# Shared experts of a mixture-of-experts layer: gate and up products for 256 tokens at a time instead of 512

## The chip, the cores and the metric

The kernel runs on one core of a Trainium2 chip. The metric is the device time of one execution in microseconds (us); lower is better. The engines are TensorE (PE in the profile, with its weight loads as PEld), VectorE (DVE), ScalarE (ACT), GpSimd (POOL) and SyncE (SP, which only starts transfers here). One wide instruction stream per engine runs in order, and the engines meet through semaphores.

## The reference, cut to what matters

A decoder layer: a state-space block, a cross-attention block and a feed-forward block, with a layer norm after each, for 8 x 128 = 1,024 tokens of width 256. Only the feed-forward block is touched:

```python
# x: 1024 tokens x 256; 8 routed experts (2 per token) and 2 shared experts, inner width 640
gate = silu(x @ wg[e].T);  up = x @ wu[e].T;  out += comb[:, e] * ((gate * up) @ wd[e].T)   # routed
sgate = silu(x @ sg[j].T); sup = x @ su[j].T; out += (sgate * sup) @ sd[j].T                # shared, all tokens
```

## The kernel before, in words

`experts` works through `NG_` = 19 groups of tokens, numbered q. Groups 0 and 1 are the first shared expert on 512 tokens each; groups 2 to 16 are the 15 routed blocks of 256 tokens (`NBLK`, `BLK` = 256); groups 17 and 18 are the second shared expert on 512 tokens each (`HALF` = 512). Every group has `IT` = 5 slices of 128 of the inner width; slice i of group q is unit u = 5q + i.

Each float32 operand is split into a high and a low part, and `products` (lines 66 to 68) makes one product of three matmuls with stationary tiles of 128 x 128: high x high, high x low, low x high. The order of the stationary operands is high, high, low, so each matmul has its weight load.

For a unit, `gate_up(q, i)` makes the gate and the up product: 2 destinations x 2 slices of the contraction (`KT`) x 3 = 12 matmuls. In a shared group each of them has 512 moving columns and fills a PSUM bank of its own (`gate_of`, `up_of`), so a unit takes two banks and units alternate between two pairs of banks. In a routed block each has 256 columns, and gate and up share a bank. Then ACT applies silu (`gate`, L1946), DVE multiplies (`gated`, L2036), ACT rounds to the high part (`round_h`), DVE makes the low part (`rest_h`), and `down(q)` makes the output, 256 columns wide: 60 matmuls in a shared group, 30 in a routed block. A unit's matmuls wait (`f_h`) until the multiply of the last unit on the same banks is done.

PE's order for each q is written out by hand: `gate_up(q, 0)`, `gate_up(q, 1)`, `down(q - 1)`, turning of a block's tokens (`turn_block`), `gate_up(q, 2)` to `gate_up(q, 4)`. In group 0, `ranks` (2 small matmuls) stands in the place of `down`, and 28 spare matmuls of 256 columns stand before `gate_up(0, 4)`. The last `down(18)` comes at the end.

GpSimd does two things in this stage: 16 indirect transfers that scatter the tokens into the blocks (L1803), once `slot` is made from the output of `ranks`, and 16 indirect transfers that gather the routed results (L1811), once the last routed results are stored. The first run beside groups 0 and 1, the second beside groups 17 and 18.

Of the kernel before, what the change touches and what calls it, by code (L numbers as in the profile page):

```python
# [24 lines left out]
KT = DM // P  # L25
HALF = 512
# [26 lines left out]
BLK = 256  # L53
NBLK = (2 * TOK + E * (BLK - 1)) // BLK
# [7 lines left out]
def products(pe, out, lhs, rhs, first, last):  # L62


    (lh, ll), (rh, rl) = lhs, rhs
    pe.matmul(out, lh, rh, start=first, stop=False)  # L66
    pe.matmul(out, lh, rl, start=False, stop=False)  # L67
    return pe.matmul(out, ll, rh, start=False, stop=last)  # L68
# [1550 lines left out]
def before_on_bank(u):  # L1619

    def banks(v):
        return (2 * (v % 2), 2 * (v % 2) + 1) if shared(v // IT) else (v % 4,)

    for v in range(u - 1, -1, -1):
        if set(banks(v)) & set(banks(u)):
            return v
    return -1


def shared(q):  # L1630
    return q < 2 or q >= 2 + NBLK


def weights_of(q):
    return 0 if q < 2 else min(q - 1, NBLK + 1)
# [7 lines left out]
def experts(nc, a, scope, ident, x_tok, accm, wr, rank, s_router, xs, ys, s_zero, out):  # L1643
# [3 lines left out]
    with ExitStack() as layer:  # L1647
        sb, ps, sem = scope(layer)
        x_hi = sb("x_hi", [P, KT, TOK], F32R)
        x_lo = sb("x_lo", [P, KT, TOK], F32R)  # L1650
# [3 lines left out]
        gu_hi = [sb(f"gu_hi{i}", [P, 2, KT, FI], F32R) for i in range(2)]  # L1654
        gu_lo = [sb(f"gu_lo{i}", [P, 2, KT, FI], F32R) for i in range(2)]
# [7 lines left out]
        xT_hi = [sb(f"xb_hi{i}", [P, KT, BLK], F32R) for i in range(2)]  # L1663
        xT_lo = [sb(f"xb_lo{i}", [P, KT, BLK], F32R) for i in range(2)]
# [60 lines left out]
        def gate_of(u):  # L1725
            return bg[2 * (u % 2)][:, :] if shared(u // IT) else bg[u % 4][:, 0:BLK]

        def up_of(u):
            return bg[2 * (u % 2) + 1][:, :] if shared(u // IT) else bg[u % 4][:, BLK:2 * BLK]

        def width(u):
            return HALF if shared(u // IT) else BLK
# [6 lines left out]
        with nc.Block() as block:  # L1739
# [82 lines left out]
            def _(pe):  # L1822
                def gate_up(q, i):
                    u, w = IT * q + i, weights_of(q)
                    c, ws = w % 2, slice(i * P, (i + 1) * P)
                    if i == 0:
                        if q < 2:
                            pe.wait_ge(r_lo, 2 * q + 2)
                        elif not shared(q):
                            pe.wait_ge(f_xlo, q - 1)  # L1830
                    if before_on_bank(u) >= 0:
                        pe.wait_ge(f_h, before_on_bank(u) + 1)
                    for dst, s in ((gate_of(u), 0), (up_of(u), 1)):
                        if i == 0:
                            pe.wait_ge(w_gl[c], 2 * (w // 2) + s + 1)
                        for k in range(KT):
                            if shared(q):
                                tok = slice((q % 2) * HALF, (q % 2 + 1) * HALF) if q < 2 else \
                                    slice((q - NBLK - 2) * HALF, (q - NBLK - 1) * HALF)
                                x2 = (x_hi[:, k, tok], x_lo[:, k, tok])  # L1840
                            else:
                                x2 = (xT_hi[q % 2][:, k, :], xT_lo[q % 2][:, k, :])
                            mm = products(pe, dst, (gu_hi[c][:, s, k, ws], gu_lo[c][:, s, k, ws]), x2, k == 0, k == KT - 1)
                    mm.then_inc(f_g, 1)

                def down(q):
# [60 lines left out]
                for q in range(4):  # L1907
                    for k in range(KT):
                        for b in range(2):
                            mm = pe.transpose(turned[q][:, k * 256 + b * P:k * 256 + (b + 1) * P],  # L1910
                                              x_tok[:, 2 * q + b, k * P:(k + 1) * P], ident[:, :])
                    mm.then_inc(r_t, 1)
                pe.wait_ge(s_router, 32)
                for b in range(BATCH):
                    pe.wait_ge(r_f, b // 2 + 1)
                    for k in range(KT):
                        mm = pe.matmul(bd[0][:, b * E:(b + 1) * E], x_f[:, k, b * P:(b + 1) * P], wr[:, k, :],  # L1917
                                       start=(k == 0), stop=(k == KT - 1))
# [3 lines left out]
                for q in range(NG_):  # L1922
                    gate_up(q, 0)
                    gate_up(q, 1)
                    if q:
                        down(q - 1)
                    else:
                        ranks()
                    if 2 <= q <= NBLK:
                        turn_block(q - 1)  # L1930
                    gate_up(q, 2)
                    gate_up(q, 3)
                    if q == 0:
                        spare(pe, bd[1][:, 0:256], x_hi[:, 0, 0:P], x_hi[:, 0, 0:256], 28)
                    gate_up(q, 4)
                    if q == 1:
                        turn_block(0)
# [369 lines left out]
```

## Time and profile before

| | |
|---|---|
| runs | 784.43 us median of 3 (784.09 to 788.73) |
| profiled execution, its own time | 784.88 us, of which the span is 783.2 us |
| PE busy | 92% of the span, 5040 matmuls |
| shared gate and up products | 240 matmuls of 128x512 (20 units x 12) |
| feed-forward stage | about 487 to 783 us of the span |

Busy time is the time in which an engine had at least one instruction under way; neighbouring matmuls overlap, so the length of one says less than the distance between the starts of two. The granted clock (PEclk) is 1.00 where TensorE runs at 2.4 GHz and 0.50 where it runs at 1.2 GHz.

### The profile page before, as it was taken

The numbers are of one execution on the slowest core, as the hardware profiler recorded it, in microseconds if no ns is written. First come the engines' busy times: TensorE is split into PE (matmuls) and PEld (weight loads), VectorE is DVE, ScalarE is ACT, GpSimd is POOL, SyncE is SP. The second block draws the span as 40 slices with busy tenths as digits, with TensorE's granted clock in tenths as the row PEclk, the third lists the DMA queues.
The fourth block names the chain that finished last, engine by engine and source line by source line (L and its number), as shares of the span: only waits on it lengthen the run. The fifth ranks groups of instructions, "written<-read, shape, count | busy, mean of one in ns | idle before, by whom it ended". The sixth has DMA issues, their size and how long they took to land. (4 is left out here: it accounts for less than half of the span.)

```text
span 783.2 us, 15336 instructions
## 1 busy us (share of the span) xinstructions
PE 723.1 (92%) x5040; PEld 655.0 (84%) x5040; DVE 565.2 (72%) x1176; ACT 473.5 (60%) x1066; POOL 347.3 (44%) x512
## 2 busy tenths in 40 slices
PE   4998888878999999999999997998999999999975
PEld 3888666667889999999899986986999999999855
DVE  4864778877878888888878873665577777777346
ACT  4544766347777777777777772343477777776301
POOL 0002666588988787877787851053000000000341
PEclk9999999999999999999999999699999999999988
DMA  9002300100200000000600000266346766770121
GB/s 293 1 1 90 160 1 0 33 3 28 62 8 1 7 0 7 0 7 0 208 0 0 0 1 5 101 225 222 119 158 227 254 200 213 229 243 28 48 74 54
DMA packets 45940, 64.82 MB, mean 83 GB/s; under 512 B 4288, under 2 KB 34880, under 8 KB 45632
## 3 DMA queue, kind: packets, MB, share of 16 engines
q1 hardware_dynamic: 39936, 56.39, 21.6%
q0 software_dynamic: 1536, 4.20, 1.6%
q10 hardware_dynamic: 4416, 3.58, 1.6%
q8 instruction: 29, 0.48, 0.3%
q14 instruction: 23, 0.19, 0.1%
HBM read 53.14 MB, written 11.01 MB: 82 GB/s over the span
## 5 line engine op out<-in xcount | busy, mean ns | idle before, releaser
L1811 POOL DMA_INDIRECT gu_raw<-rows_out,slot x16 | 15.9, 995 | 203.1 <-DMA rows_out<-y_sb 198.5
L1946 ACT ACTIVATE sg<-bg 128x256 f32<-128x256 f32 (+1 forms) x95 | 40.8, 430 | 101.6 <-PE bg L68 87.5
L413 ACT ACTIVATE under_dt<-two,nb,under_raw 128x256 f32<-128x256 f32 x128 | 70.6, 561 | 45.5 <-DVE nb L496 45.5
L66 PE MATMUL bg<-xb_hi,gu_hi 128*128 128x256 f32 x300 | 86.9, 290 | 2.7 <-DVE xb_lo L2059 2.7
L2036 DVE TENSOR_TENSOR hf<-sg,bg 128x256 f32<-128x256 f32 (+1 forms) x95 | 45.0, 474 | 57.4 <-ACT sg L1946 53.8
L68 PE MATMUL bg<-xb_hi,gu_lo 128*128 128x256 f32 x300 | 85.6, 285 | 0.0
L67 PE MATMUL bg<-xb_lo,gu_hi 128*128 128x256 f32 x300 | 85.5, 285 | 0.0
L66 PE MATMUL two<-under_h 128*128 128x256 f32 (+1 forms) x208 | 66.9, 321 | 2.8 <-PEq L117 1.5
L594 POOL TENSOR_SCALAR under_dt<-under_dt,rec 128x256 f32<-128x256 f32 x128 | 62.7, 508 | 6.4 <-DVE rec L542 6.4
L66 PE MATMUL bd<-dn_hi,eh_hi 128*128 128x256 f32 x220 | 62.5, 284 | 1.9 <-issue 1.8
L67 PE MATMUL bd<-dn_lo,eh_hi 128*128 128x256 f32 x220 | 62.6, 285 | 1.6 <-issue 1.6
L68 PE MATMUL bd<-dn_hi,eh_lo 128*128 128x256 f32 x220 | 62.3, 283 | 1.5 <-issue 1.5
L66 PEld LDWEIGHTS bg<-xb_hi,gu_hi 128*128 128x128 f32 x300 | 58.2, 194 | 3.1 <-DVE xb_lo L2059 3.1
L2048 DVE TENSOR_TENSOR gu_lo<-gu_raw,gu_hi 128x1280 fp32r<-128x1280 f32 x34 | 50.5, 1488 | 12.6 <-ACT gu_hi L1961 12.6
L67 PE MATMUL two<-under_h 128*128 128x256 f32 (+1 forms) x208 | 58.7, 282 | 0.0
L68 PE MATMUL two<-under_h 128*128 128x256 f32 (+1 forms) x208 | 58.5, 281 | 0.0
L68 PEld LDWEIGHTS bg<-xb_hi,gu_lo 128*128 128x128 f32 x300 | 58.2, 194 | 0.0
L67 PEld LDWEIGHTS bg<-xb_lo,gu_hi 128*128 128x128 f32 x300 | 58.2, 194 | 0.0
L546 DVE TENSOR_TENSOR pT_lo<-two,pT_hi 128x1024 fp32r<-128x1024 f32 x32 | 39.2, 1225 | 21.2 <-ACT pT_hi L420 21.0
L1953 ACT ACTIVATE eh_hi<-hf 128x256 fp32r<-128x256 f32 (+1 forms) x95 | 43.2, 455 | 11.3 <-DVE hf L2036 9.7
L2042 DVE TENSOR_TENSOR eh_lo<-hf,eh_hi 128x256 fp32r<-128x256 f32 (+1 forms) x95 | 45.3, 477 | 2.9 <-ACT eh_hi L1953 0.3
L66 PEld LDWEIGHTS bd<-dn_hi,eh_hi 128*128 128x128 f32 x220 | 42.2, 192 | 2.9 <-issue 2.6
(294 smaller groups left out, 2556.5 us busy)
## 6 DMA issues: line engine op xcount, KB each, us to landing
gu_raw<-in_gu SPq DMA_DIRECT2D x17, 1280.0 KB
dn_raw<-in_dn SPq DMA_DIRECT2D x17, 640.0 KB
rows_in<-under_dt SPq DMA_DIRECT2D x1, 3840.0 KB, 13.1
rows_out<-y_sb SPq DMA_DIRECT2D x30, 128.0 KB, 2.1
x_blk<-rows_in ACTq DMA_DIRECT2D x13, 256.0 KB, 2.7
under_raw<-in_wq SPq DMA_DIRECT2D x1, 2048.0 KB, 7.7
under_raw<-in_wkv SPq DMA_DIRECT2D x1, 2048.0 KB, 12.3
under_raw<-in_wo SPq DMA_DIRECT2D x4, 512.0 KB, 4.0
```

The costliest lines, as they stand in the source:

```text
L66: pe.matmul(out, lh, rh, start=first, stop=False)
L67: pe.matmul(out, lh, rl, start=False, stop=False)
L68: return pe.matmul(out, ll, rh, start=False, stop=last)
L413: act.activation(self.prob[:, g % 2, h, :], self.b_s[:, h // 2, (h % 2) * MW:(h % 2 + 1) * MW], ACT.Exp, bias=self.nb[:, h:h + 1], scale=s ...
L546: dve.tensor_tensor(self.pT_lo[:, :, :], self.b_p[:, :, :], self.pT_hi[:, :, :].bitcast(F32), ALU.subtract).then_inc(self.a_plo, 1)
L594: pool.tensor_scalar(self.prob[:, g % 2, h, :], self.prob[:, g % 2, h, :], self.rec[:, h:h + 1], 1.0, ALU.mult, ALU.mult).then_inc(self.a_ ...
L1811: pool.indirect_dma_start(got[k][:, b, :], None, ys[:, :], bass.IndirectOffsetOnAxis(ap=slot[:, k, b:b + 1], axis=0)).then_inc(f_got[b], 16)
L1946: act.activation(sg[:, u % 3, 0:width(u)], gate_of(u), ACT.Silu).then_inc(f_sg, 1)
L1953: act.activation(h_hi[:, q % 2, i, 0:width(u)], hf[:, u % 3, 0:width(u)], ACT.Copy).then_inc(f_hhi, 1)
L2036: dve.tensor_tensor(hf[:, u % 3, 0:width(u)], sg[:, u % 3, 0:width(u)], up_of(u), ALU.mult).then_inc(f_h, 1)
L2042: dve.tensor_tensor(h_lo[:, q % 2, i, 0:n], hf[:, u % 3, 0:n], h_hi[:, q % 2, i, 0:n].bitcast(F32), ALU.subtract).then_inc(f_hlo, 1)
L2048: dve.tensor_tensor(gu_lo[c][:, s, :, :], gu_raw[c][:, s, :, :], gu_hi[c][:, s, :, :].bitcast(F32), ALU.subtract).then_inc(w_gl[c], 1)
```

## The change

In `gate_up`, the unit's tokens are cut into parts of `BLK` = 256 and the products are made part by part: for a shared unit first all of gate's contraction for the first 256 tokens (6 matmuls into the first half of gate's bank), then for the second 256, then the same for up. A shared unit then has 24 matmuls of 256 columns with 24 weight loads in place of 12 of 512 with 12. The banks, the semaphore increments, the waits, and all work of ACT, DVE, POOL and SP stay as they are. A routed unit has one part and is issued as before.

```diff
-                        for k in range(KT):
-                            if shared(q):
-                                tok = slice((q % 2) * HALF, (q % 2 + 1) * HALF) if q < 2 else \
-                                    slice((q - NBLK - 2) * HALF, (q - NBLK - 1) * HALF)
-                                x2 = (x_hi[:, k, tok], x_lo[:, k, tok])
-                            else:
-                                x2 = (xT_hi[q % 2][:, k, :], xT_lo[q % 2][:, k, :])
-                            mm = products(pe, dst, (gu_hi[c][:, s, k, ws], gu_lo[c][:, s, k, ws]), x2, k == 0, k == KT - 1)
+
+                        for part in range(width(u) // BLK):
+                            for k in range(KT):
+                                if shared(q):
+                                    at = (q if q < 2 else q - NBLK - 2) * HALF + part * BLK
+                                    x2 = (x_hi[:, k, at:at + BLK], x_lo[:, k, at:at + BLK])
+                                else:
+                                    x2 = (xT_hi[q % 2][:, k, :], xT_lo[q % 2][:, k, :])
+                                mm = products(pe, dst[:, part * BLK:(part + 1) * BLK],
+                                              (gu_hi[c][:, s, k, ws], gu_lo[c][:, s, k, ws]), x2, k == 0, k == KT - 1)
                     mm.then_inc(f_g, 1)
```

## Rows read from the trace of the kernel before

**Rows 1.** The page: PE's busy time, and the queue that carries instruction blocks.
```profile
PE 723.1 (92%) x5040; PEld 655.0 (84%) x5040; DVE 565.2 (72%) x1176; ACT 473.5 (60%) x1066; POOL 347.3 (44%) x512
...
q8 instruction: 29, 0.48, 0.3%
```
**Rows 2.** The tile bg: count, ns minimum/median/maximum, first and last start.
```profile
L66 PE MATMUL bg<-xb_hi,gu_hi x300: 278/283/415, 546.2 to 719.7; 128*128 128x256 f32 x150
...
L66 PE MATMUL bg<-x_hi,gu_hi x80: 387/389/790, 501.0 to 767.1; 128*128 128x512 f32 x80
```
**Rows 3.** Busy time by stretch: from:to, its length, engines, PEclk, DMA share, GB/s.
```profile
514.40:531.50 17.10, 16.47 (x105) 14.80 (x103) 11.33 (x17) 8.11 (x11) 13.74 (x12) 1.00 0.88 314
531.50:540.40 8.90, 8.10 (x35) 5.53 (x33) 3.53 (x6) 0.77 (x2) 4.79 (x5) 1.00 0.25 86
540.40:546.20 5.80, 3.48 (x16) 2.68 (x16) 3.26 (x7) 3.07 (x6) 0.00 (x0) 1.00 0.95 325
...
563.30:720.00 156.70, 156.70 (x1312) 156.70 (x1313) 120.14 (x197) 114.27 (x223) 0.00 (x0) 1.00 0.60 197
720.00:736.00 16.00, 16.00 (x88) 13.85 (x87) 5.22 (x10) 5.71 (x12) 0.00 (x0) 1.00 0.06 19
736.00:748.40 12.40, 12.40 (x78) 11.23 (x77) 8.50 (x16) 4.11 (x8) 9.63 (x10) 1.00 0.30 87
748.40:757.40 9.00, 3.77 (x15) 2.18 (x13) 2.55 (x6) 0.00 (x0) 6.30 (x7) 0.85 0.38 107
757.40:761.60 4.20, 4.17 (x10) 3.00 (x11) 1.51 (x4) 0.00 (x0) 0.00 (x0) 0.50 0.06 22
```
**Rows 4.** PE in order of time: wide products, then narrow ones, without a gap.
```profile
519.05 0.39 PE L68 MATMUL bg<-x_hi,gu_lo 128*128 128x512 f32 x1
...
525.17 0.39 PE L68 MATMUL bg<-x_hi,gu_lo 128*128 128x512 f32 x1
...
525.75 0.28 PE L66 MATMUL bd<-dn_hi,eh_hi 128*128 128x256 f32 x1
...
531.15 0.28 PE L66 MATMUL bd<-dn_hi,eh_hi 128*128 128x256 f32 x1
```
**Rows 5.** PE in order of time, groups 0 and 1, idle time in brackets.
```profile
517.11 0.50 PE L66 MATMUL bg<-x_hi,gu_hi 128*128 128x512 f32 x1 [0.63 <-DVE hf L2036]
...
533.06 0.48 PE L66 MATMUL bg<-x_hi,gu_hi 128*128 128x512 f32 x1
...
537.38 0.39 PE L68 MATMUL bg<-x_hi,gu_lo 128*128 128x512 f32 x1 [0.23 <-issue]
...
538.81 0.40 PE L67 MATMUL bg<-x_lo,gu_hi 128*128 128x512 f32 x1
...
540.50 0.50 PE L66 MATMUL bg<-x_hi,gu_hi 128*128 128x512 f32 x1 [0.36 <-DVE hf L2036]
```
**Rows 6.** POOL in order of time: first and last indirect transfer, scatter and gather.
```profile
514.38 2.53 POOL L1803 DMA_INDIRECT rows_in<-x_tok,slot  x1 [26.26 <-DVE slot L2147]
...
536.54 0.96 POOL L1803 DMA_INDIRECT rows_in<-x_tok,slot  x1 [0.30 <-issue]
...
736.03 0.99 POOL L1811 DMA_INDIRECT gu_raw<-rows_out,slot  x1 [198.53 <-DMA rows_out<-y_sb]
...
755.58 0.95 POOL L1811 DMA_INDIRECT gu_raw<-rows_out,slot  x1 [0.30 <-issue]
```
**Rows 7.** PE in order of time, beginning and end of the stretch at 1.2 GHz.
```profile
757.43 0.79 PE L66 MATMUL bg<-x_hi,gu_hi 128*128 128x512 f32 x1 [0.33 <-issue]
...
761.59 0.40 PE L66 MATMUL bg<-x_hi,gu_hi 128*128 128x512 f32 x1
```
**Rows 8.** The chain that ended last, where group 1 ends and group 2 begins.
```profile
543.31 0.25 PE bg L68
...
546.21 0.39 PE bg L66
```
**Rows 9.** DMA queues in the stretch 563.3 to 720: packets, MB, share.
```profile
q8 instruction: 11, 0.18, 0.5%
```

## The prediction

> **What bounds the kernel now.** I read the page first: PE is busy for 92% of the span [rows 1], so the question is what PE's own stream costs. The tile view then says which instructions the change touches: the wide products, 80 for each of three lines, 240 in all [rows 2]. Third came a table by stretch [rows 3]. In the routed stretch PE and its weight loads are busy for all of the 156.70 us. The same holds for 720 to 748.4. PE is the bound there, and a longer PE stream moves the end one for one. Three stretches look different. In 531.5 to 540.4 PE handles 35 matmuls in 8.90 us; in 748.4 to 757.4 it handles 15 in 9.00 us; in 757.4 to 761.6 the granted clock is 0.50. The reader should see that the first two lie under the last part of POOL's two runs of indirect transfers, 514.38 to 537.50 and 736.03 to 756.53 [rows 6], and that PE's gaps there are put down to "issue": it waited for no semaphore. Where group 1 hands over to group 2, the chain runs from PE's last product through ACT and DVE and back to PE in 2.9 us [rows 8], so a later end of group 1 is passed on in full.
>
> **The plain price.** The length of one matmul (389 ns wide, 283 ns narrow [rows 2]) is no price, because neighbours overlap. The distance of starts is. Wide: from 519.05 to 525.17 there are 27 steps, 6.12 / 27 = 0.2267 us. Narrow: from 525.75 to 531.15 there are 45 steps, 5.40 / 45 = 0.1200 us [rows 4]. Two narrow ones cost 0.2400, so each wide product that is cut costs 0.0133 us more, and 240 cost 3.2 us. The weight loads double from 240 to 480 and add nothing to this: the narrow rows already have one load each.
> The Trainium skill, TensorE: Matmul & The Clock Gate, section Back-to-back issue gap, gives columns / 2.4 + 2.5 ns for a single stream of matmuls; an estimate by that page is 2.5 ns for each cut and 0.6 us for all 240. The trace differs: its fixed part is five times as large, with a weight load for each matmul. I go by the trace.
>
> Two corrections. First, at 517.11 PE waits 0.63 us for DVE's multiply [rows 5], whose engine is behind because it makes the tokens' places from the output of `ranks`. The 24 wide products ahead of `ranks` move that chain by 0.32 us; the 48 ahead of 517.11 move PE by 0.64. So about 0.3 of 0.64 us arrives. Second, the products at clock 0.50 (10 in 4.20 us [rows 3], 757.43 to 761.59 [rows 7]) take 0.42 us each; at half the clock two narrow ones should cost the same, so 0.1 us falls away. The plain price is 3.2 - 0.3 - 0.1 = 2.8 us. DVE and ACT have the same work and gain slack. The 0.36 us wait at 540.50 [rows 5] could hide a little more; I leave that in the range.
>
> **What the plain price leaves out: instructions.** PE's instruction count in the shared gate and up products doubles, from 480 to 960 with the weight loads, and the question is whether they arrive as fast as PE could use them. The routed stretch says yes when POOL is quiet: 1312 matmuls in 156.70 us, 8.4 per us [rows 3]. While POOL issues indirect transfers, the rows say no. Between 533.06 and 540.50 PE does the 24 wide products of two units [rows 5]; less the closing wait and the tail before it, that is about 6.9 us against 24 x 0.2267 = 5.4. PE pauses in a rhythm of 1.43 us (537.38, 538.81 [rows 5]), with about 5 products in each: 24 / 6.9 = 3.5 products per us. The narrow rate wanted by the change is 8.3. In the gather it is worse: 13 or so in 9.00 us, 1.4 per us [rows 3].
> Why did neither pause begin with the indirect transfers? A store that is emptied explains it. Before 531.5 PE had done about 101 products since 514.4 (14 spare, 36 wide, 51 narrow); before 748.4 it had done 77 since 736.0 (30 wide, 47 narrow: 30 x 0.2267 + 47 x 0.12 = 12.4). With 3.5 per us arriving, 101 - 60 = 41 and 77 - 43 = 34 came out of the store. The two agree roughly, which is why I take this seriously; it is an inference, since no row shows the store.
>
> *Scatter.* From 517.1 to 540.4 PE did 36 wide, 60 narrow and 24 wide: 120 products. The same place now needs 72 + 60 + 48 = 180. Upper bound: the store is emptied in both kernels, the same 120 arrive, and 60 narrow ones are left when the supply recovers: 60 x 0.12 = 7.2 us. Lower bound: the shortage begins at 531.5 whatever PE has used. Then PE reaches 117 of 132 by 531.5, 33 more arrive by 540.4, and 30 are left: 3.6 us. The last unit of the group adds 0.2.
> *Gather.* Before, 90 products by 757.4. Now 120 are needed. Upper bound: the same 90 arrive, 30 x 0.12 = 3.6 us. Lower: the shortage begins at 748.4 again, by then 103 of 120 are done, 13 arrive, 4 are left: 0.5 us.
> *Elsewhere.* 0.3 us before the scatter; 720 to 736 holds (16.00 - 30 x 0.12) / 0.2267 = 55 wide products, 0.7 us; the end, 27 warm ones, 0.4 us.
> *Clock.* A narrow product occupies PE half as long as a wide one, so at 3.5 per us PE is idle for more than half of the time, as it was before the clock fell to 0.50 at 757.4. A second such stretch after the scatter would cost up to 16 narrow products at about 0.21 instead of 0.12 us, 1.5 us; at least nothing, because the kernel before already has a slow start after 546.2.
>
> Sum: low 0.3 + 3.8 + 0.7 + 0.5 + 0.4 = 5.7 us; high 0.3 + 7.4 + 0.7 + 3.6 + 0.4 + 1.5 = 13.9 us. Between them I take 10: the agreement of the two stores speaks for the upper half, and an argument from two stretches for some caution. 784.9 + 10 = 794.9 for the profiled execution; it lies 0.45 us above the median, so 794.5 us. This case's own range is 790 to 799.
> The Trainium skill, Runtime: NRT & Kernel Launch, section Instruction fetch mechanics, says that instructions are streamed in blocks ahead of use and that this is mostly hidden. By that page the forecast would be the plain price. The routed stretch agrees with it; the two stretches under POOL's transfers don't, unless the pauses have another cause.
>
> **Rivals.**
> *A. Only the plain price.* The pauses are tied to POOL's transfers in time and not to how many instructions PE uses; then 784.4 + 2.8 = 787.2 us, 786 to 789.5. For it: under the 30 wide products after 736.0 nothing pauses, though the transfers run. Against it: five products for each 1.43 us looks like a count. Chance 0.28.
> *B. The forecast*, 790 to 799. Chance 0.50.
> *C. The scatter starves as hard as the gather did.* At 1.4 per us from the start of a shortage at about 525, 15 us bring 21 products where the upper bound has 53, 32 x 0.12 = 3.8 us on top of 13.9: about 801 to 804. For it: the gather's rate is a row. Against it: the scatter's own rate is 3.5. Chance 0.08.
> *D. Faster: the gather's shortage moves away.* Instructions come in blocks on queue 8, 11 for the 1312 + 1313 of the routed stretch [rows 3, 9], about 240 in each. The change puts 240 more instructions ahead of the gather's groups and 240 into them. If the shortage arises where PE comes to the end of a block while POOL is busy, then what decides is whether such an end lies between 736 and 757; groups 17 and 18 shift by about one block, which nearly restores the old place, so only a difference of some tens of instructions could move it out. If it does, the 13 products of 9.00 us take 1.6, and the 10 at half clock take 2.3 instead of 4.20: 9.3 us less, 784.4 + 2.8 - 9.3 = 778 us. With only a part of it gone the time is 778 to 784. Chance 0.10.
> *E. The change does nothing to PE*, because the second load of the same weights or the split of the bank hides something: no row points to it, and the time would be 784. Chance 0.04.
>
> **How the numbers follow.** A measurement of this kernel tells a change of about 1% from none, 776.6 to 792.3 us. Below it lies a part of D, 0.03. Within: A, E, most of D, and about 0.13 of B, 0.51. Above: 0.37 of B, and C, 0.46. The likeliest single case is still B, with 794.5. The range has to take in A and B, and runs from 785.5 to 800; it leaves out C, D, E and edges, 0.2.
>
> **What would show it.** In the profile after: 480 narrow matmuls from x_hi and x_lo on bg, 0.120 us apart where nothing else happens (if not, the plain price is wrong); 31 packets on queue 8 instead of 29; PE's first pause after 514 well before 531, in the middle of `down(0)` or earlier, with "issue" as its releaser (if it comes at 531 to 532, the store is wrong and the low sum stands; if there is none, A); the end of group 1 4 to 9 us later than 543.6 on PE; the routed stretch of 156.70 us unchanged; from the gather's first transfer to the end of `down(17)` 1 to 4 us longer. The prediction is wrong if PE issues 8 products per us beside POOL's transfers, or if the pauses move with block ends rather than with what has been used.

## The result and the profile after

The changed kernel takes 800.11 us (median of 4 runs, 795.65 to 805.16), the kernel before 784.26 us on the same chip. The ratio is 1.0177 with a 95% interval of 1.0125 to 1.0229, that is 13.9 us slower (784.3 x 0.0177). The four runs fall into two pairs, 795.65 and 796.31, 803.9 and 805.16, and the median lies between them. The profiled execution is one of the longer pair, 805.16 us with a span of 802.4 us; its 19.2 us over the span before are more than the typical difference. Three kernels of the experiments had one execution each at a much lower granted clock (976.93, 822.39 and 825.17 us), which is left out of their times and ratios here.

The page, PE and the queue of instruction blocks [rows 1]:

```profile
PE 732.1 (91%) x5280; PEld 674.9 (84%) x5280; DVE 564.1 (70%) x1176; ACT 473.5 (59%) x1066; POOL 344.3 (43%) x512
...
q8 instruction: 30, 0.49, 0.3%
```

The tile bg, the products on x_hi [rows 2]; there were 80 of 512 columns for each line:

```profile
L66 PE MATMUL bg<-x_hi,gu_hi x160: 277/283/415, 502.8 to 786.6; 128*128 128x256 f32 x160
```

Busy time by stretch, as in [rows 3]. The columns are from:to, length, PE, PEld, DVE, ACT, POOL (busy us and instructions), granted clock, DMA share, GB/s.

```profile
516.90:529.20 12.30, 11.94 (x99) 11.74 (x98) 6.00 (x12) 2.98 (x5) 9.86 (x9) 1.00 0.84 292
529.20:541.10 11.90, 4.84 (x17) 3.58 (x16) 0.52 (x1) 0.00 (x0) 7.10 (x8) 0.63 0.57 211
541.10:559.30 18.20, 15.92 (x114) 15.67 (x113) 11.44 (x17) 8.96 (x13) 0.00 (x0) 0.86 0.46 150
...
576.70:733.20 156.50, 156.50 (x1312) 156.50 (x1311) 119.83 (x196) 114.19 (x222) 0.00 (x0) 1.00 0.60 197
...
751.00:762.00 11.00, 10.09 (x81) 9.64 (x80) 4.53 (x8) 2.35 (x4) 8.56 (x9) 1.00 0.32 96
762.00:771.50 9.50, 2.39 (x8) 1.46 (x7) 5.51 (x11) 1.75 (x3) 6.98 (x7) 0.63 0.34 97
771.50:780.00 8.50, 6.65 (x38) 6.83 (x39) 1.51 (x4) 0.00 (x0) 0.00 (x0) 0.61 0.06 18
```

Its second row is to be read first: in 529.2 to 541.1 PE handled 17 matmuls in 11.9 us. Before, it handled 35 in 8.9. POOL's indirect transfers, first and last of the scatter and of the gather [rows 6]:

```profile
516.89 2.53 POOL L1803 DMA_INDIRECT rows_in<-x_tok,slot  x1 [26.46 <-DVE slot L2149]
...
537.48 0.96 POOL L1803 DMA_INDIRECT rows_in<-x_tok,slot  x1 [0.31 <-issue]
...
750.97 0.99 POOL L1811 DMA_INDIRECT gu_raw<-rows_out,slot  x1 [212.53 <-DMA rows_out<-y_sb]
...
770.16 0.95 POOL L1811 DMA_INDIRECT gu_raw<-rows_out,slot  x1 [0.30 <-issue]
```

PE in order of time. The two pauses that answer to [rows 5] and [rows 7], with the idle time in brackets:

```profile
529.07 0.28 PE L66 MATMUL bd<-dn_hi,eh_hi 128*128 128x256 f32 x1
529.74 0.28 PE L67 MATMUL bd<-dn_lo,eh_hi 128*128 128x256 f32 x1 [0.38 <-issue]
...
534.02 0.37 PE L67 MATMUL bd<-dn_lo,eh_hi 128*128 128x256 f32 x1 [1.04 <-issue]
...
541.14 0.37 PE L67 MATMUL bd<-dn_lo,eh_hi 128*128 128x256 f32 x1 [0.43 <-issue]
...
545.59 0.41 PE L67 MATMUL bd<-dn_lo,eh_hi 128*128 128x256 f32 x1
...
760.97 0.38 PE L68 MATMUL bd<-dn_hi,eh_lo 128*128 128x256 f32 x1 [0.43 <-issue]
...
773.73 0.37 PE L68 MATMUL bd<-dn_hi,eh_lo 128*128 128x256 f32 x1 [1.03 <-issue]
```

The first pause beside the scatter now comes after the 7th product of `down(0)`, 12.8 us after POOL's first transfer. Before, the hesitation began near the 51st, 17 us after. From 541.3 to 546.0 products are about 0.213 us apart, with no idle time between them: the instructions come again, but the granted clock is still 0.50.

Where the 19.2 us are. Each row below is the distance between four starts read from the tile view and PE's order of time: first shared product, first routed product, first product of group 17, last matmul, and from that to the end of the span.

| us | first product at | groups 0, 1 | routed | groups 17, 18 | tail |
|---|---|---|---|---|---|
| before | 501.0 | 45.2 | 173.9 | 54.7 | 8.4 |
| after | 502.8 | 56.5 | 174.0 | 60.7 | 8.4 |
| difference | 1.8 | 11.3 | 0.1 | 6.0 | 0.0 |

The first column lies ahead of the change: the first product starts anywhere from 497.6 to 502.8 in the profiles of kernels that are the same up to it. The change itself costs 11.3 us beside the scatter and 6.0 beside the gather in this execution. The profiles of the other kernels that have GpSimd's transfers, described below, bear this out: groups 0 and 1 take 44.4 to 50.2 us wide and 54.6 to 56.6 narrow. Groups 17 and 18, in the order of before and with all transfers, take 54.7 to 57.9 wide and 58.4 to 60.7 narrow.

### The profile page after: what moved, and what is told of

It is laid out like the page before. It is cut to its first block and busy times, and to the rows that moved or that the text cites. A ratio compares the mean times of both kernels' runs of the same rounds, so it can differ in the third digit from the quotient of the medians.

```text
span 802.4 us, 15816 instructions
## 1 busy us (share of the span) xinstructions
PE 732.1 (91%) x5280; PEld 674.9 (84%) x5280; DVE 564.1 (70%) x1176; ACT 473.5 (59%) x1066; POOL 344.3 (43%) x512
## 5 line engine op out<-in xcount | busy, mean ns | idle before, releaser
L1811 POOL DMA_INDIRECT gu_raw<-rows_out,slot x16 | 15.6, 973 | 217.1 <-DMA rows_out<-y_sb 212.5
L2038 DVE TENSOR_TENSOR hf<-sg,bg 128x256 f32<-128x256 f32 (+1 forms) x95 | 45.1, 475 | 79.5 <-ACT sg L1948 71.8
L67 PE MATMUL bd<-dn_lo,eh_hi 128*128 128x256 f32 x220 | 65.0, 295 | 6.4 <-issue 6.3
L66 PE MATMUL bd<-dn_hi,eh_hi 128*128 128x256 f32 x220 | 64.9, 295 | 6.5 <-issue 6.5
L68 PE MATMUL bd<-dn_hi,eh_lo 128*128 128x256 f32 x220 | 64.8, 295 | 4.0 <-issue 4.0
L2050 DVE TENSOR_TENSOR gu_lo<-gu_raw,gu_hi 128x1280 fp32r<-128x1280 f32 x34 | 50.6, 1490 | 12.7 <-ACT gu_hi L1963 12.7
L67 PEld LDWEIGHTS bd<-dn_lo,eh_hi 128*128 128x128 f32 x220 | 44.7, 203 | 7.7 <-issue 7.7
L66 PEld LDWEIGHTS bd<-dn_hi,eh_hi 128*128 128x128 f32 x220 | 44.6, 203 | 6.0 <-issue 6.0
L68 PEld LDWEIGHTS bd<-dn_hi,eh_lo 128*128 128x128 f32 x220 | 44.7, 203 | 5.7 <-issue 5.7
```

The costliest lines, as they stand in the source:

```text
L1811: pool.indirect_dma_start(got[k][:, b, :], None, ys[:, :], bass.IndirectOffsetOnAxis(ap=slot[:, k, b:b + 1], axis=0)).then_inc(f_got[b], 16)
L2038: dve.tensor_tensor(hf[:, u % 3, 0:width(u)], sg[:, u % 3, 0:width(u)], up_of(u), ALU.mult).then_inc(f_h, 1)
L2050: dve.tensor_tensor(gu_lo[c][:, s, :, :], gu_raw[c][:, s, :, :], gu_hi[c][:, s, :, :].bitcast(F32), ALU.subtract).then_inc(w_gl[c], 1)
```

## The experiments

My theory: while GpSimd issues indirect transfers, hardly any instructions reach PE, which lives on a store of them; narrow products use the store up sooner. The rivals: the transfers' traffic is the cause, whoever starts it; the pauses come at the ends of instruction blocks (rival D of the prediction); the pauses come at a fixed time; narrow products are dear by themselves.

**Who starts the transfers.** In two kernels GpSimd's 32 indirect transfers are left out, and SyncE moves the same bytes in a fixed order of rows (the tokens are not routed):

```diff
-  pool.indirect_dma_start(xs[:, :], bass.IndirectOffsetOnAxis(ap=slot[:, k, b:b + 1], axis=0),
-                          x_tok[:, b, :], None).then_inc(r_scat, 16)
+  sp.dma_start(xs[n * P:(n + 1) * P, :], x_tok[:, b, :]).then_inc(r_scat, 16)      # n = 2 * b + k
...
-  pool.indirect_dma_start(got[k][:, b, :], None, ys[:, :], bass.IndirectOffsetOnAxis(...))
+  sp.dma_start(got[k][:, b, :], ys[n * P:(n + 1) * P, :])
```

With wide products:

> Wide products as before. The 16 scatter and 16 gather transfers of GpSimd are left out; SyncE moves the same bytes at the same places in the program, in a fixed order of rows, so the routing of tokens is left out. Theory 1 (PE lives on a store of instructions that hardly fills while GpSimd issues indirect transfers): no pause of PE with the releaser issue in groups 0, 1, 17 and 18, the clock stays at 1.00 there, and the time falls by 8 to 12 us, to 773 to 776 us. Theory 2 (the traffic of the transfers itself holds PE's instructions up, whoever starts them): pauses of several us remain and the time stays above 780 us.

Measured: 773.58 us, ratio 0.9868 (0.9831 to 0.9906), 10.3 us faster than before. With narrow products:

> Narrow products in the shared groups, with the same replacement of GpSimd's transfers by SyncE's (the routing is left out). Theory 1: no pauses here either; the difference to the wide kernel with the same replacement is the plain price alone, 2 to 4 us. Theory 2 (traffic): 8 us or more between the two. A third view, that narrow products are slower for a reason of their own that the 0.120 us does not show, would also give well over 4 us.

Measured: 775.17 us, ratio 0.9879 (0.9846 to 0.9912). By the ratios the two differ by 0.9 us, less than the 2 to 4 that I expected; each ratio is known to about 3 us, which leaves room for the plain price but not for the 8 us of the traffic theory. All waits of PE from 500 us to the end, in the narrow kernel's view of waits (waiting tile, releaser: us, times, longest):

```profile
PE bg L66 <- DVE xb_lo L2062: 2.7, 2, 2.2
PE bg L66 <- DVE hf L2039: 0.4, 1, 0.4
```

No wait has the releaser "issue", neither here nor in the wide one. The stretch in which SyncE issues the scatter's 16 transfers (515.74 to 524.21), and the one after it, in which weights and blocks are loaded:

```profile
515.70:525.00 9.30, 8.94 (x74) 8.74 (x74) 6.37 (x14) 2.95 (x5) 0.00 (x0) 1.00 0.68 224
525.00:543.00 18.00, 18.00 (x152) 18.00 (x151) 10.26 (x15) 7.55 (x10) 0.00 (x0) 1.00 0.97 339
```

PE loses 0.36 of the 9.30 us, to the wait for VectorE in the list above, and does 152 matmuls in 18.00 us with the DMA engines 97% busy. Before, PE paused while they were 25% busy (531.5 to 540.4 [rows 3]). So the amount of traffic is not what holds PE up; GpSimd's indirect transfers are. The pair changes three things at once, who starts the transfers, their indirect form, and their pace (SyncE issues 16 in 8.5 us, GpSimd in 22), and no run separates these. That narrow products are dear by themselves also falls: groups 0 and 1 take 43.7 us wide and 44.1 narrow, groups 17 and 18 take 45.1 and 46.7.

**Half of the change each.** One condition decides which groups are cut:

```diff
+  n = BLK if q <= NBLK + 1 else width(u)      # groups 0 and 1 (or: q >= 2, groups 17 and 18)
-  for part in range(width(u) // BLK):
+  for part in range(width(u) // n):            # and n in place of BLK in the slices below
```

> Narrow products in groups 0 and 1 only, wide ones in 17 and 18. Theory 1: PE's pauses in the scatter begin near 529 as in the changed kernel, and the time is 7 to 12 us above before, 791 to 797 us; the gather stretch looks as before. If both halves cost the same, 8 us; if the price were only the plain one, 1.4 us.

Measured: 794.73 us, ratio 1.0136 (1.0069 to 1.0203), 10.6 us by the ratio. Groups 0 and 1 take 56.5 us, the same as with the whole change, groups 17 and 18 take 55.1.

> Narrow products in groups 17 and 18 only, wide ones in 0 and 1. Theory 1: the store is empty about 9 us after the first gather transfer instead of 12, about 30 products are left when the supply recovers, partly at half clock: 4 to 7 us above before, 788 to 792 us. Plain price only: 1.6 us. The sum of this and of the kernel with narrow products in groups 0 and 1 only should be the whole change, 14 to 18 us.

Measured: 786.7 us, ratio 1.0044 (1.0003 to 1.0084), 3.4 us. Groups 0 and 1 take 45.6, groups 17 and 18 take 58.4. That is less than I expected (4 to 7), though the interval, 0.2 to 6.6 us, reaches into it. The ratios add up to 1.0180 against 1.0177 for the whole. Such close agreement is luck, since the ratios are known to 0.004 and 0.007, but it gives no sign that the halves act on each other. The larger part of the price lies beside the scatter, 10.6 of 13.9 us by the ratios and 11.3 of 17.3 in the profile.

**Count, time or block ends.** More spare products ahead of group 0 push all later instructions of PE on without altering what PE does beside the transfers:

```diff
-  spare(pe, bx[1][:, 0:256], x_hi[:, 0, 0:P], x_hi[:, 0, 0:256], 16)
+  spare(pe, bx[1][:, 0:256], x_hi[:, 0, 0:P], x_hi[:, 0, 0:256], 80)      # or 48
```

> The kernel before with 64 more spare products of 256 columns ahead of group 0 (80 instead of 16), so that all later instructions of PE lie half an instruction block further on, while what PE does beside GpSimd's transfers stays the same. Theory 1a (a store of about fixed size when the transfers begin): the pauses begin again about 17 us after the first scatter transfer and 12 us after the first gather transfer, with 87 and 76 matmul records between, and the time is 7.7 us (64 x 0.12) above before, about 791. Theory 1b (the store ends at the end of an instruction block): both beginnings move by up to 64 products, and the time differs from 791 by several us either way.

Measured: 790.15 us, ratio 1.0092 (1.0045 to 1.0140), 7.2 us against the 7.7 of the products themselves.

> The same with 32 more spare products. Theory 1a: pauses begin as before (17 and 12 us after the first transfer), time 3.8 us above before, about 787. Theory 1b: both beginnings move by about 32 products against before, in the same direction as with 64 and half as far.

Measured: 792.62 us (two runs), ratio 1.0114 (1.0051 to 1.0178), 8.9 us instead of the 3.8 expected; the interval begins at 4.0. Its profile shows where they are: groups 0 and 1 take 50.2 us, 5.0 more than before, in pauses beside the scatter, and groups 17 and 18 take 57.9.

> The changed kernel with 64 more spare products ahead of group 0. Theory 1a: pauses begin 12 us after the first scatter transfer and 9 us after the first gather transfer, as in the changed kernel, time 7.7 us above it, about 808 us. Theory 1b: the beginnings move by tens of products.

Measured: 809.54 us (two runs), ratio 1.0330 (1.0263 to 1.0397), 12.0 us above the changed kernel's ratio, with 8 expected; the intervals of the two ratios are wide enough for that.

What separates the theories is where the pauses begin. From PE's and POOL's order of time, counted from POOL's first transfer of the gather to PE's first start that comes more than 0.22 us later than due, without a wait for VectorE:

| kernel | after the first transfer | matmul records between |
|---|---|---|
| before (wide) | 12.9 us | 77 |
| narrow in 0 and 1 only (wide here) | 14.9 | 81 |
| wide, 64 more | 14.2 | 80 |
| wide, 32 more | 12.1 | 70 |
| after (narrow) | 9.3 | 75 |
| narrow in 17 and 18 only | 12.2 | 95 |
| narrow, 64 more | 10.0 | 76 |
| late order, mended, wide (below) | 18.7 | 87 |
| the same with 14 wide spare products (below) | 18.0 | 87 |
| late order, mended, narrow (below) | 11.6 | 89 |
| narrow, half of the gather (below) | 10.1 | 81 |

At the wide rate of 4.4 products per us 75 products would take 17 us, at the narrow rate 9; the time spreads from 9.3 to 18.7 us, a factor of two, the count from 70 to 95. The two kernels of the mended late order, which differ in width alone, pause after 18.7 and 11.6 us but after 87 and 89 records. So in the gather the count fits better than a fixed time, though it is no constant: the same narrow program gives 75 and 95.

Moving the program on by a quarter or half a block of about 240 instructions moves neither time nor count in a consistent direction, so block ends don't set them. Queue 8 says the same. I number PE's matmul and weight-load records by their starts. In the changed kernel a block comes at 747.4 us behind about 10,540 records, the next at 774.8 behind about 10,790; in the SyncE twin the same two come at 733.4 and 748.3, behind as many records. So while the changed kernel pauses in the gather (760.3 to 773.7) no block is on its way or later in PE's program than without pauses, and PE runs on at 773.9, before the next one. Over the eleven kernels of the table the first pause lies anywhere from 68 to 251 records behind the last block. Whatever PE lacks there, it is not a block of queue 8.

Beside the scatter the five kernels with narrow products there pause first after 12.7 to 12.9 us, each with 78 to 80 records and the 16 to 18 spare products that were running when the transfers began: 96 to 98 products. Since these kernels issue the same products there, time and count can't be told apart by them; the 64 more spare products of one of them move neither, which speaks against block ends here too. Of the seven with wide ones and GpSimd's transfers, four pause first after 15.6 to 17.0 us (78 to 93 products), the kernel before hesitates from 17 us on and is first late by that measure after 21.6 (122 products), one, with 64 more spare products, after 24.2 (135), and one (the late order, below) never. So with wide products neither a count nor a time explains the scatter, since kernels with the same program up to there (before, and the late order) differ; the expectation of 17 us for the shifted wide kernel missed there.

**The order of PE's work.** If the store is what counts, narrow work beside the gather should be put off. This kernel, wide, issues `down(17)` after the last three units of group 18:

```diff
   gate_up(q, 0)
   gate_up(q, 1)
-  if q:
+  if q and q != NG_ - 1:
       down(q - 1)
...
+  down(NG_ - 2)
   down(NG_ - 1)
```

VectorE's `add_last` and `norm_stats` of the first four tiles move behind its last multiply, and the last group's output banks are taken in another order.

> The kernel before (wide products) with one other order: down(17), 60 narrow products, is issued after the last three gate and up units of group 18 instead of before them, so that PE does 66 wide products first while GpSimd gathers; VectorE's additions of the first half of the output and their norms move behind its last multiply. Theory 1 (a store emptied by count): after the first gather transfer about 77 to 93 products are done before the first pause, that is not before 15 us of the 21 us, and few pauses are left: 3 to 8 us faster than before, 776 to 780 us. If the pauses begin at a fixed time after the first transfer, whatever PE issues, the time stays within 2 us of before or is worse.

Measured: 783.58 us, ratio 1.0013 (0.9983 to 1.0043). The expected gain is missing, for a reason that the order of time shows, first PE's, then VectorE's of the same stretch:

```profile
748.10 0.39 PE L68 MATMUL bg<-x_hi,gu_lo 128*128 128x512 f32 x1
754.70 0.80 PE L66 MATMUL bg<-x_hi,gu_hi 128*128 128x512 f32 x1 [6.22 <-issue]
...
753.04 1.01 DVE L2171 SCALAR_TENSOR_TENSOR acc<-gu_raw,share,acc 128x256 f32<-128x256 f32 x2 [1.45 <-issue]
753.97 1.28 DVE L2039 TENSOR_TENSOR hf<-sg,bg 128x512 f32<-128x512 f32 x2
```

The label "issue" misleads here. VectorE's additions of gathered rows (`mix`) wait for the gather, and the multiply that frees PE's banks is queued behind them; PE starts at 754.70, at once when the first of the two multiplies is done (754.65). Until 748.10 this kernel had no late start, for 53 records; what the count would have brought after them is hidden by the wait. The mended order, with those additions behind the multiplies:

```diff
   gated(IT * q)
-  if last:
-      mix(0); mix(1)
   gated(IT * q + 1)
...
-  if last:
-      for b in range(2, 6): mix(b)
+  if last:
+      mix(0); mix(1)          # mix(2), mix(3) after gated(IT * q + 3), the rest after the norm's statistics
```

> As the kernel with down(17) issued late, mended: there PE stood still for 6.2 us because VectorE's additions of gathered rows were queued ahead of the multiply that frees PE's banks. Now they stand behind it: rows of two token tiles after the third unit of group 18, of two more after the fourth, the rest after the last. Theory 1 (a store of about 75 to 95 products that hardly fills): PE does 66 wide products in the first 15 us of the gather and 10 to 30 narrow ones before the first pause, so pauses last at most 4 us instead of 9 and the clock falls for a shorter time: 5 to 9 us faster than before, 774 to 778 us. If PE's supply simply stops some 12 us after the first transfer, pauses fall into the wide products and at most 2 us are won.

Measured: 783.56 us, ratio 0.998 (0.995 to 1.001). No difference can be told. In its profile PE's first late start (752.49) comes 18.7 us after the first transfer (733.78) instead of 12.9:

```profile
751.42 0.28 PE L66 MATMUL bd<-dn_hi,eh_hi 128*128 128x256 f32 x1
752.49 0.28 PE L67 MATMUL bd<-dn_lo,eh_hi 128*128 128x256 f32 x1 [0.79 <-issue]
...
756.94 0.42 PE L67 MATMUL bd<-dn_lo,eh_hi 128*128 128x256 f32 x1
...
759.72 0.41 PE L68 MATMUL bd<-dn_hi,eh_lo 128*128 128x256 f32 x1
```

Groups 17 and 18 take 51.5 us instead of 54.7, and 1.5 of the 3.2 are given back in the tail (9.9 instead of 8.4), where VectorE now has the additions that it had put off. Of the 5 to 9 us that I expected, 1.7 are there in this profile, which is less than the runs can show. The pauses did move as the count foretold; that the kernel would gain by it was wrong.

> The late wide order, and the 28 narrow spare products of group 0 replaced by 14 of 512 columns, which hold PE for 0.2 us less and need half as many instructions. Theory 1: some 7 products fewer are drawn from the store beside the scatter, whose pauses cost 1 to 5 us in the wide kernels; 0 to 2 us less than the late wide order, 772 to 778 us.

```diff
-  spare(pe, bd[1][:, 0:256], x_hi[:, 0, 0:P], x_hi[:, 0, 0:256], 28)
+  spare(pe, bd[1][:, 0:512], x_hi[:, 0, 0:P], x_hi[:, 0, 0:512], 14)
```

Measured: 783.94 us, ratio 0.998 (0.9956 to 1.0004), the same as without that edit, and 6 us above the range expected. Beside the scatter the first pause comes 15.6 us after the first transfer in both, with 86 products without the edit and 78 with it: saving spare products put nothing off, which a count alone would not give. The narrow twin of the mended order:

> The same order with narrow products in the shared groups. Theory 1: 132 narrow products stand in the 16 us in which the late wide order needs 66 wide ones; the first pause comes again 9 to 12 us after the first gather transfer, 75 to 95 records on, now inside gate and up products of group 18, and the time is within 3 us of the changed kernel, 797 to 803 us. If it were down's own products that starve (another place in memory, another bank), the gate and up products would run through and the time would fall by 8 us.

Measured: 802.54 us, ratio 1.0237 (1.0186 to 1.0287). PE's pauses, now among gate and up products:

```profile
754.27 0.28 PE L67 MATMUL bg<-x_lo,gu_hi 128*128 128x256 f32 x1 [0.69 <-issue]
755.69 0.28 PE L66 MATMUL bg<-x_hi,gu_hi 128*128 128x256 f32 x1 [1.01 <-issue]
...
766.35 0.58 PE L66 MATMUL bg<-x_hi,gu_hi 128*128 128x256 f32 x1 [7.03 <-DVE hf L2041]
```

The first comes 11.6 us and 89 records after the first transfer (742.66), inside the count's range. So it is not `down` in particular that starves. The 7.03 us are again a wait for VectorE.

**How long it lasts.** The changed kernel with one gather transfer per tile instead of two (the rows of each token's second expert are left out, old contents take their place; VectorE's wait for each tile is halved to match):

```diff
   for b in range(BATCH):
-      for k in range(2):
+      for k in range(1):
           pool.indirect_dma_start(got[k][:, b, :], None, ys[:, :], ...)
```

> The changed kernel (narrow) with only 8 of the 16 gather transfers, those of each token's first expert; the second expert's rows are left out (old contents are added in their place). Theory 1: GpSimd is done 10 us after the first gather transfer, about when the store is empty, so the pauses in group 17's down nearly vanish and the time falls by 9 to 13 us against the changed kernel, to 787 to 791 us. If each transfer had a price for PE of its own, it would fall by half of that.

Measured: 789.59 us, ratio 1.0074 (1.0044 to 1.0103), 8.1 us less than the changed kernel by the ratios, where I expected 9 to 13. The two intervals leave that difference uncertain by some 5 us, so the runs alone don't decide between the two theories. POOL's last transfer, and PE's pauses:

```profile
758.30 0.94 POOL L1811 DMA_INDIRECT gu_raw<-rows_out,slot  x1 [0.30 <-issue]
...
759.40 0.37 PE L67 MATMUL bd<-dn_lo,eh_hi 128*128 128x256 f32 x1 [0.20 <-issue]
760.11 0.28 PE L68 MATMUL bd<-dn_hi,eh_lo 128*128 128x256 f32 x1 [0.34 <-issue]
760.83 0.37 PE L66 MATMUL bd<-dn_hi,eh_hi 128*128 128x256 f32 x1 [0.45 <-issue]
```

The profile does decide: groups 17 and 18 take 48.3 us instead of 60.7, and groups 0 and 1 take 56.5 in both. Leaving out the last half of the transfers took away all but 1.6 of the 11.9 us of late starts in the gather. So a transfer has no fixed price for PE: the first eight cost nearly nothing, and those that come after PE's first pause cost nearly all. The pauses end 1.6 us after POOL's last transfer is done here (760.8 against 759.2), 2.6 us after it in the changed kernel (773.7 against 771.1).

## Why the prediction was right

The direction and the place held, and so did the kind of mechanism: PE runs short beside GpSimd's transfers, and earlier when its products are narrow. The size was at the upper end. Forecast 794.5 us, range 785.5 to 800. On the 784.43 us from which it started the measured ratio gives 798.3; the median of the changed kernel, 800.11, lies a tenth of a us above the range, and two of its four runs lie well above. That the typical time stayed at the edge owes something to luck: in the profiled execution each of the two places exceeded its upper bound, together 17.3 us against a high sum of 13.9.

*The plain price.* 0.120 us between narrow starts held [rows 4]. It was put at 2.8 us; in the pair without GpSimd's transfers it is 0.4 us in groups 0 and 1 and 1.5 in groups 17 and 18, the latter being 120 x 0.0133 = 1.6. In groups 0 and 1 more of it fell into waits for VectorE than I had allowed (late starts of 0.8 and 0.3 us wide, 0.5 narrow), and the stretch at half clock at the start ended 2.0 us after the first shared product in the narrow kernel and 2.5 us after it in the wide one.

*PE runs short beside GpSimd's transfers.* That the pauses need them is shown by the pair with SyncE in GpSimd's place: all pauses go, wide and narrow. That what runs short is instructions, from a store, is inferred from the releaser "issue" and from the count in the gather. Beside the scatter the count is not shown: time does as well for narrow products, and for wide ones neither does.

*Scatter, 3.6 to 7.2 us, with the clock up to 8.7.* This was the mis-sized term: with the plain price before it and the last unit, groups 0 and 1 could cost 9.2 us at most, and they measured 11.3 in the profile. The end of group 1 on PE came 11.5 us later, not counting the later start, where I had named 4 to 9 as the sign. I took the supply from the kernel before, 3.5 products per us. In the changed kernel it was 15 products in 11.9 us, 1.3 per us, the gather's rate. So the mechanism of rival C, to which I gave 0.08, is the one that the trace shows, and its time, 801 to 804, is as near to 800.11 as my own case's 790 to 799. I had set it aside because the scatter's own rate was a row; but that row came from a stretch where PE was pausing only a little, and says little of the rate once pauses are long. At half clock 22 products from 541.3 to 546.0 cost about 22 x 0.093 = 2.0 us more than at full clock, a little above the 1.5 I allowed. A small slip besides: at 3.5 per us the 8.9 us of the lower bound bring 31 products, not 33.

*Gather, 0.5 to 3.6 us.* With the plain price around it the high sum gave groups 17 and 18 4.7 us; they cost 6.0 in the profile. Of these 1.8 lie ahead of the first transfer, 0.7 of plain price and the rest because GpSimd began about 8 products later in PE's order. From the first transfer to the last matmul it went from 774.81 - 736.03 = 38.8 to 794.00 - 750.97 = 43.0 us, 4.2 more, which includes the 0.5 of plain price after it. The upper bound was the right one for this pair: about as many products are done when the supply recovers, 90 before and 88 after, and what is left has to be done afterwards. It is no rule, since the kernel with narrow products in 17 and 18 only had done 113. The two values that I had worked out for the store, 41 and 34 products with 3.5 per us arriving, were wrong together: with about 1 per us arriving, the same two counts give 65 to 85. I also read the rows too well in one place: from 720 to 748.4 PE is busy all the time, but its weight loads are not (13.85 of 16.00 and 11.23 of 12.40 us [rows 3]); no term rests on it.

*Rivals.* A (plain price only, 787.2) is refuted, since the pauses begin earlier and last longer with narrow products; it holds only in the pair without GpSimd's transfers. D (block ends) is refuted for the gather by the shifted kernels and by queue 8. E (no effect) is refuted. The routed stretch was unchanged, as said (156.5 for 156.7 us). Queue 8 shows 30 packets within the span where I said 31; a 31st comes 2 us behind its end. That count was the weakest of the signs. The Trainium skill, Runtime: NRT & Kernel Launch, section Instruction fetch mechanics, says that streaming in blocks is mostly hidden. The trace agrees as far as blocks go: in the SyncE pair PE never waits with the releaser "issue", and in the changed kernel's gather queue 8 owes PE no block while it pauses. I had read the sentence as a statement on the whole supply of instructions, and the pauses beside indirect transfers lie outside of what it speaks of.

*What stays open.* How GpSimd's indirect transfers hold up PE, and, if it is instructions that PE lacks, where they wait after queue 8 has brought them; whether the indirect form, GpSimd as the starter, or the pace is what matters; and why wide kernels with the same program up to the scatter's end begin to pause there anywhere from 15.6 to 24 us after the first transfer, or not at all. No view shows the store itself.

## What to carry to other kernels

Where a profile puts PE's idle time down to "issue", look at what GpSimd does then: beside the gather here PE did 70 to 95 products, each with its weight load, and then about one to two per us until GpSimd was done. Don't cut instructions in two there: that cost 10.6 us by the ratio beside the scatter. Do not expect as much from the reverse, since putting narrow work off and halving the number of spare products gained nothing that the runs can tell; what gained was to have no indirect transfers (1.3%). Read the rate of a shortage only from a stretch in which pauses are long, and before trusting the word "issue", check that no other engine's queue stands between PE and its banks.

## What the runs showed of the hardware

Replacing 32 indirect transfers of GpSimd by SyncE's of the same bytes, in fixed rows, gained 1.3% (0.9 to 1.7) without touching PE's program. Matmuls and weight loads are equally many in every profile, also where the stationary tile stays the same: 64 more spare products on one tile brought 64 more weight loads (5104 of each instead of 5040). During a shortage PE's starts come in steps of about 0.71 or 1.42 us: 530.48, 531.88, 532.61, 534.02 in the changed kernel. A product of 512 columns and one of 256 differ by 0.107 us in the distance of starts, so each has a fixed 0.013 us, if the rest goes by columns. The Trainium skill, TensorE: Matmul & The Clock Gate, section Back-to-back issue gap, has a fixed part of 0.0025 us in its formula for an isolated matmul, and for pairs of weight load and matmul, which is the case here, it gives about 131 ns at 512 columns; the trace has 226.7 ns. During and after a shortage the granted clock is 0.50 for some us (757.4 to 761.6 before): 0.213 us between narrow starts, 0.43 between wide ones.
